# Graph stage: ELUs as relu plus residual plus a clamped exponential, and a row by transposes instead of a matrix product

## What is computed

```python
def _gat(inp, adj_mask, W, a):
    h = jnp.matmul(inp, W)
    f1 = jnp.matmul(h, a[:F_, 0]); f2 = jnp.matmul(h, a[F_:, 0])
    e = jax.nn.leaky_relu(f1[:, :, None] + f2[:, None, :], ALPHA)
    if adj_mask is not None:
        e = jnp.where(adj_mask[None, :, :] > 0, e, NEG_INF)
    att = jax.nn.softmax(e, axis=2)
    return jax.nn.elu(jnp.einsum('bij,bjf->bif', att, h))
out = jax.nn.relu(jnp.matmul(x, mlp1_w) + mlp1_b); residual = out
out = _gat(jax.nn.relu(out), None, W_fc, a_fc)            # 256 features
out = jax.nn.elu(out) + residual
out = jax.nn.relu(jnp.matmul(out, mlp2_w) + mlp2_b); residual = out
out = _gat(jax.nn.relu(out), adj, W_hand, a_hand)         # 128 features
out = jax.nn.elu(out) + residual
return jax.nn.relu(out)
```

## Time and profile before

| | |
|---|---|
| runs, us | 1070.05, 1070.69, 1064.08; median 1070.05 |
| profiled execution, span us | 1059.3 |
| busy, us and share of the span | PE 927.0 (88%), DVE 717.5 (68%), ACT 661.1 (62%), POOL 504.2 (48%) |
| graph stage: b_rden of slot 0 and of slot 13 | 700.4 and 918.4 us from the span's start |
| pace of most full slots | 16.7 us |

### The profile page before, as it was taken

The page is one execution under the profiler, slowest core; times in us unless marked ns, Lnnn a source line. Parts: engine busy times, 40 slices in busy tenths (PEclk is TensorE's granted clock), DMA queues, the critical chain, the costliest instruction groups (busy, mean ns, idle before and its releaser), DMA issues. The chain is left out here.

```text
span 1059.3 us, 25141 instructions
## 1 busy us (share of the span) xinstructions
PE 927.0 (88%) x8021; PEld 805.6 (76%) x8021; DVE 717.5 (68%) x2252; ACT 661.1 (62%) x1691; POOL 504.2 (48%) x498
## 2 busy tenths in 40 slices
PE   1799998999899999999998994798898888768997
PEld 1588887887688999999998993466565666548896
DVE  4599888988464135555554544579898888678775
ACT  4556665654544546666665662688888888867652
POOL 2566564663035564444444442576767732244340
PEclk9999998999699999999999996999999999978999
DMA  7913221211354216777676861011111100000112
GB/s 195 371 50 122 120 109 70 114 42 54 101 148 131 65 49 194 212 202 197 198 200 173 210 162 33 23 33 34 32 35 28 35 6 1 1 1 20 41 42 60
DMA packets 93007, 103.59 MB, mean 98 GB/s; under 512 B 16352, under 2 KB 69856, under 8 KB 90720
## 3 DMA queue, kind: packets, MB, share of 16 engines
q1 hardware_dynamic: 73232, 59.78, 17.3%
q10 hardware_dynamic: 11472, 25.63, 9.0%
q0 software_dynamic: 8192, 16.79, 5.5%
HBM read 52.60 MB, written 43.27 MB: 91 GB/s over the span
## 5 line engine op out<-in xcount | busy, mean ns | idle before, releaser
L1319 POOL DMA_INDIRECT slot_rows_in<-xn_all,slots x128 | 130.1, 1016 | 142.7 <-DMA slot_rows_in<-xn_all,slots 105.8
L1205 ACT ACTIVATE s_hT<-s_hp,expert 128x256 f32<-128x256 f32 x284 | 111.5, 476 | 52.4 <-PE s_hp L1196 52.4
L1218 PE MATMUL s_yp<-w_experts,s_hT 128*128 x1136 | 138.0, 275 | 0.0
L1218 PEld LDWEIGHTS s_yp<-w_experts,s_hT 128*128 128x128 f32 x1136 | 132.8, 192 | 0.0
L1226 DVE TENSOR_TENSOR xnT_all<-s_yp,expert 128x256 f32<-128x256 f32 x71 | 30.2, 425 | 117.9 <-PE s_yp L1218 114.7
L489 DVE SCALAR_TENSOR_TENSOR l_mi<-l_sbc,mT 128x512 bf16<-128x512 f32 x128 | 84.3, 668 | 4.0 <-PE l_sbc L480 3.3
L1194 PE MATMUL s_hp<-e_xh,e_wh 128*128 128x256 f32 x284 | 85.9, 303 | 0.0
L1196 PE MATMUL s_hp<-e_xh,e_wl 128*128 128x256 f32 x284 | 80.1, 282 | 0.0
L1195 PE MATMUL s_hp<-e_xl,e_wh 128*128 128x256 f32 x284 | 80.1, 282 | 0.0
L1176 ACT CAST e_wh<-expert 128x512 fp32r<-128x512 f32 x71 | 43.9, 619 | 48.8 <-issue 43.1
L1120 ACT ACTIVATE s_hT<-s_hp,b_shared 128x512 f32<-128x512 f32 x64 | 42.8, 688 | 48.4 <-PE s_hp L1091 47.2
(11 more groups left out here) (353 smaller groups left out, 2701.0 us busy)
## 6 DMA issues: line engine op xcount, KB each, us to landing
expert<-expert_rows ACTq DMA_DIRECT2D x65, 322.0 KB, 3.4
slot_rows_in<-zeros SPq DMA_DIRECT2D x9, 1024.0 KB, 12.2
xnT_all<-slot_rows_in SPq DMA_DIRECT2D x71, 128.0 KB, 3.4
slot_rows_out<-xnT_all SPq DMA_DIRECT2D x71, 128.0 KB, 2.8
slot_rows_out<-zeros SPq DMA_DIRECT2D x8, 1024.0 KB, 4.4
xn_all<-l_xr SPq DMA_DIRECT2D x16, 256.0 KB, 2.3
xnT_all<-l_rT SPq DMA_DIRECT2D x16, 256.0 KB
out_dram<-xn_all SPq DMA_DIRECT2D x16, 256.0 KB, 2.3
```

The source lines that it names most:

```text
L1205: nc.scalar.activation(hT[q % 2][:, c, :], hp[:, c, 0:TILE], ACT.Gelu, bias=wt[q][:, F + c:F + c + 1]).then_inc(s["h_ok"], 1)
L1218: ins = pe.matmul(yp[q % 2][:, h * D:(h + 1) * D], hT[q % 2][:, c, h * P:(h + 1) * P], w2, start=(c == 0 and h == 0), stop=(c == FC - 1), ...
L1319: pool.indirect_dma_start(k.rows_in, bass.IndirectOffsetOnAxis(ap=k.slots[:, c, b:b + 1], axis=0), k.xn[:, b, :], None).then_inc(scattered ...
```

## The change

Both double ELUs with their residual r are written as max(q, 0) + r + min(exp(exp(q) - 1), 1), which is 1 too much. The cuts of v1 and v2 ahead of the second exponential go. In stage c, DVE does `dve_c_linear` (z1 = max(mm, 0) + r1T) and later `dve_c_sum` (u1 = min(w1, 1) + z1), and POOL's residual goes. In stage e, DVE does `dve_e_sum` (z2 = max(q2, 0) + rr) and `dve_e_out` (s2 = min(w2, 1) + z2). The 1 too much is taken back by constants: mlp2's bias minus the sum of its weights' rows (two small products in `pe_table`, one subtraction), max(s2, 1) for the relu, and -1 in the experts' second bias.

f2 becomes column 129 of h2 (W2C = D + 2), and `pe_d_f2` makes the row from it by four transposes of a broadcast column, after h2 is copied by ACT.

Orders change. DVE's slot now begins e_sum, e_out, c_linear, leaky of d, n_apply, c_sum. ACT does y2's sum after v1 instead of ahead of the rstd step. PE does f2 after `pe_b_sums`, in slot C after the last layer's compaction and row transposes. PE's next writes to `mm` wait for z1 instead of t1.

```diff
-            dve.tensor_scalar(v1[:], v1[:], 1.0, None, ALU.min).then_inc(s["v1_cut"], 1)
...
+        def dve_c_linear(dve, g, p):
+            wait(dve, s["u1_ok"], g)
             wait(dve, s["v1_ok"], g + 1)
+            dve.scalar_tensor_tensor(z1[:], mm[:], 0.0, r1T[p][:], ALU.max, ALU.add).then_inc(s["z1_ok"], 1)
+        def dve_c_sum(dve, g):
+            wait(dve, s["r2_ps"], g)
+            wait(dve, s["z1_ok"], g + 1)
             wait(dve, s["w1_ok"], g + 1)
-            dve.scalar_tensor_tensor(t1[:], w1[:], -1.0, mm[:], ALU.add, ALU.max).then_inc(s["t1_ok"], 1)
-            pool.tensor_tensor(u1[:], t1[:], r1T[p][:], ALU.add).then_inc(s["u1_ok"], 1)
+            dve.scalar_tensor_tensor(u1[:], w1[:], 1.0, z1[:], ALU.min, ALU.add).then_inc(s["u1_ok"], 1)
...
-            pe.matmul(ff[:], k.w_f2_hand[:], r2T[p][:], start=True, stop=True).then_inc(s["f2_ps"], 1)
+            wait(pe, s["h2_ok"], g + 1)
+            for b in range(GB):
+                ins = pe.transpose(ff[:, b * P:(b + 1) * P], h2[:, b, D + 1:D + 2].to_broadcast([P, P]), k.ident[:])
...
-            dve.tensor_scalar(v2[:], v2[:], 1.0, None, ALU.min).then_inc(s["v2_cut"], 1)
+        def dve_e_sum(dve, g):
+            dve.scalar_tensor_tensor(z2[:], q2[:], 0.0, as_batches(rr[:]), ALU.max, ALU.add).then_inc(s["z2_ok"], 1)
         def dve_e_out(dve, g):
-            dve.scalar_tensor_tensor(t2[:], w2[:], -1.0, q2[:], ALU.add, ALU.max).then_inc(s["t2_ok"], 1)
-            dve.tensor_tensor(s2[:], t2[:], as_batches(rr[:]), ALU.add).then_inc(s["s2_ok"], 1)
+            wait(dve, s["x_ok"], g)
+            wait(dve, s["z2_ok"], g + 1)
             wait(dve, s["w2_ok"], g + 1)
+            dve.scalar_tensor_tensor(s2[:], w2[:], 1.0, z2[:], ALU.min, ALU.add).then_inc(s["s2_ok"], 1)
...
         def pe_slot(pe, g, half, p, on):
             if on["d"]:
                 pe_d_h2(pe, g, p)
-                pe_d_f2(pe, g, p)
             if g == C:
                 last.pe_compact(pe, 0)
                 last.pe_row(pe, 1)
+                pe_d_f2(pe, g)
...
             if on["c"]:
                 pe_b_sums(pe, g + 1, q)
+            if on["d"] and g < C:
+                pe_d_f2(pe, g)
...
         def dve_slot(dve, g, half, p, on):
             if on["e"]:
-                dve_e_cut(dve, g - 1)
+                dve_e_sum(dve, g - 1)
+            if on["e"]:
+                dve_e_out(dve, g - 1)
+            if on["c"]:
+                dve_c_linear(dve, g + 1, q)
             if on["d"]:
                 dve_d_leaky(dve, g)
-            if on["c"]:
-                dve_c_cut(dve, g + 1)
             if on["a"]:
                 dve_n_apply(dve, g + 3, q)
             if on["c"]:
-                dve_c_max(dve, g + 1)
-            if on["e"]:
-                dve_e_out(dve, g - 1)
+                dve_c_sum(dve, g + 1)
```

More of the change, by code:

```diff
@@ L1038, in experts_phase @@
         READ_PREFIX = 16
+        W2_SUM = 80
         SPLIT = 2
@@ L1071, in pe_table @@
             pe.transpose(counts[0:EC, 16:16 + J], last_of[:], k.ident[0:J, 0:J])
+            for c in range(2):
+                pe.matmul(counts[:, W2_SUM:W2_SUM + 1], k.w_mlp2[:, c, :], k.ones[:, 0:1], start=(c == 0),
+                          stop=(c == 1), skip_group_check=True)
             for e in range(EXPERTS + 1):
@@ L1541 @@
 W1S = FD + 4
-W2C = D + 1
+W2C = D + 2
 def last_ffn_steps(nc, ctx, k, out, bank, graph, tail_of):
@@ L1659, in pe_row @@
         if g == 0:
-            pe.wait_ge(graph["t1_ok"], GROUPS)
+            pe.wait_ge(graph["z1_ok"], GROUPS)
         wait(pe, s["rank_ok"], g)
@@ L1773, in pe_out @@
         if g < 2:
-            pe.wait_ge(graph[("q2_ok", "s2_ok")[g]], GROUPS)
+            pe.wait_ge(graph[("q2_ok", "z2_ok")[g]], GROUPS)
         wait(pe, s["out_ok"], g - 1)
@@ L1940, in graph_and_last_phase @@
         p1T = sb("p1T", [P, GB * P])
-        v1, w1, t1, u1 = (sb(n, [P, H1, GB * P]) for n in ("v1", "w1", "t1", "u1"))
+        v1, w1, z1, u1 = (sb(n, [P, H1, GB * P]) for n in ("v1", "w1", "z1", "u1"))
         r2T = [sb(f"r2T{p}", [P, GB * P]) for p in range(2)]
@@ L1947, in graph_and_last_phase @@
         p2T = sb("p2T", [P, GB * P])
-        q2, v2, w2, t2, s2 = (sb(n, G4) for n in ("q2", "v2", "w2", "t2", "s2"))
+        q2, v2, w2, z2, s2 = (sb(n, G4) for n in ("q2", "v2", "w2", "z2", "s2"))
         tb = ps("tb", [P, 512])
@@ L2039, in pe_a_dense @@
         def pe_a_dense(pe, g):
-            wait(pe, s["t1_ok"], g - 1)
+            wait(pe, s["z1_ok"], g - 1)
             wait(pe, s["r1_ok"], g * H1)
@@ L2047, in act_a_r1 @@
         def act_a_r1(act, g, p):
-            wait(act, s["u1_ok"], g - 1)
+            wait(act, s["z1_ok"], g - 1)
             for c in range(H1):
@@ L2128, in pe_b_sums @@
             wait(pe, s["r1_ok"], full(lambda n: n * H1, g, 1))
-            wait(pe, s["t1_ok"], g)
+            wait(pe, s["z1_ok"], g)
             wait(pe, s["p1T_ok"], g + 1)
@@ L2142, in act_c_exp, with act_c_exp2 @@
             nc.scalar.activation(v1[:], mm[:], ACT.Exp).then_inc(s["v1_ok"], 1)
-        def dve_c_cut(dve, g):
-            wait(dve, s["v1_ok"], g + 1)
-            dve.tensor_scalar(v1[:], v1[:], 1.0, None, ALU.min).then_inc(s["v1_cut"], 1)
[L2148 to L2154, removed]
-            wait(dve, s["w1_ok"], g + 1)
-            dve.scalar_tensor_tensor(t1[:], w1[:], -1.0, mm[:], ALU.add, ALU.max).then_inc(s["t1_ok"], 1)
-        def pool_c_residual(pool, g, p):
-            wait(pool, s["r2_ps"], g)
-            wait(pool, s["t1_ok"], g + 1)
-            pool.tensor_tensor(u1[:], t1[:], r1T[p][:], ALU.add).then_inc(s["u1_ok"], 1)
+        def act_c_exp2(act, g):
+            wait(act, s["u1_ok"], g)
+            wait(act, s["v1_ok"], g + 1)
+            nc.scalar.activation(w1[:], v1[:], ACT.Exp, bias=k.neg_one[:]).then_inc(s["w1_ok"], 1)
+        def dve_c_linear(dve, g, p):
+            wait(dve, s["u1_ok"], g)
+            wait(dve, s["v1_ok"], g + 1)
+            dve.scalar_tensor_tensor(z1[:], mm[:], 0.0, r1T[p][:], ALU.max, ALU.add).then_inc(s["z1_ok"], 1)
+        def dve_c_sum(dve, g):
+            wait(dve, s["r2_ps"], g)
+            wait(dve, s["z1_ok"], g + 1)
+            wait(dve, s["w1_ok"], g + 1)
+            dve.scalar_tensor_tensor(u1[:], w1[:], 1.0, z1[:], ALU.min, ALU.add).then_inc(s["u1_ok"], 1)
         def pe_c_dense(pe, g):
-            wait(pe, s["s2_ok"], g - 1)
+            wait(pe, s["z2_ok"], g - 1)
             wait(pe, s["r2_ok"], g)
@@ L2242, in pe_d_r2 @@
             wait(pe, s["r2_ok"], full(lambda n: n, g, 1))
-            wait(pe, s["s2_ok"], g)
+            wait(pe, s["z2_ok"], g)
             for b in range(GB):
@@ L2261, in dve_e_quotient @@
         def dve_e_quotient(dve, g, p):
-            wait(dve, s["t2_ok"], g)
+            wait(dve, s["v2_ok"], g)
+            wait(dve, s["z2_ok"], g)
             wait(dve, s["rden2_ok"], g + 1)
@@ L2354, in act_slot @@
                 act_c_exp(act, g + 1)
+            if on["d"]:
+                act_d_sum(act, g)
             if g == B:
```

37 lines of the change are left out of this document (16 added, 21 removed), and 2 rows, old and new, of the table s.

## The result

The change makes the kernel slower: median 1085.99 us (1080.1 to 1091.4, four runs) against 1069.01 us for the kernel before measured beside it (1064.08 to 1070.69), a ratio of 1.0162 with a 95% interval of 1.0115 to 1.021. That is 17.0 us; the forecast was +12.7 and 1082.5. All ratios here leave out runs in a slower state: one of 1078.01 us of the kernel before, and one of 1524.08 us, at a granted clock of 0.564, of the variant with n_apply early. The profiled execution spans 1086.7 us, 27.4 more than that of before, so part of what it shows (some 10 us) isn't the change. The busy times of the page hardly move: PE 925.8, DVE 718.6, ACT 661.8 us, POOL 460.7 for 504.2. So the loss has to be in waits, that is in the pace of the slots.

The account below looks back on a forecast made before the run. No engine is full; a loop through DVE's n_apply, PE and ACT sets the slot. Terms 14.0 + 1.2 - 1.0 - 1.1 - 0.8 + 0.4 = +12.7 on 1070.05 give 1082.75, called 1082.5; range 1068 to 1089, own range 1077 to 1087.

Parts of the forecast that it names:

- slots 1 to 12: Steady graph slots: 16.73 us each becomes 17.96, so 201.48 us becomes 215.5, +14.0.
- slot 0: Graph slot without stage e; c_linear ahead of its leaky group and y2's later sum cost a steady slot's +1.2 us.
- slot -1: Graph slot ahead of slot 0: leaky 1 falls from 1.70 to 0.7 us, -1.0.
- slot 13: Graph slot without n_apply: leaky 1 loses 0.8 us and ACT is 0.3 earlier by the missing cut, -1.1.
- slots 14, 15 and the last phase: Graph stage's end: earlier c_dense gains 2.0 us, slot 15 gives it back; one fewer DVE step in last phase, -0.8.
- experts, start of the graph stage: Experts stage: two small matrix products more cost between 0 and 0.6 us, taken as +0.4.
- rival 3: In 12 slots, e_out with two SBUF inputs waits out 1.0 us of POOL's work: 1094 us, chance 0.16.
- DVE waits for nothing here, with at least 0.15 us to spare: DVE's steps ahead of n_apply: w2, v1 and y2's sum from ACT each arrive before DVE needs them.
- The median of the runs is 10.75 above the span: Whole run: the median's excess over the profiled span of 1059.3 us was taken as unchanged, giving a base of 1070.05.
- Rival 1: Graph slots: c_dense sets the pace, so PE's 0.48 us wait for POOL comes back in 16 slots: 1060, chance 0.10.
- Rival 2: Price paid, but less: cheap c_linear, and PE's clock staying up after shorter idleness wins 2.3 us: 1075, chance 0.16.
- Rival 4: Graph slots: n_apply is later but unseen DVE slack hides it, only the ends (-3) count: 1067 us, chance 0.09.

Follow-up runs that it names:

- the variant with n_apply early: The kernel before with the new ELUs only, DVE doing leaky of d and n_apply ahead of c_linear, e_sum and e_out: 1063.98 us, ratio 0.9932.
- the clean pair: Second profiled executions of the unchanged kernels before and after, on one chip, neither with a late signal: 1058.96 and 1077.11 us, spans 1057.0 and 1075.1.

## Why the prediction was right, and where it was off

**The mechanism held.** DVE's work ahead of n_apply set the pace, PE's wait for n_apply appeared (1.49 us), and leaky 1 takes 0.69 everywhere with 2.93 us of idleness ahead of it. Taking n_apply out from behind the new work, with nothing else changed, gave it all back (16.47 in slots without gathers).

**The slot: 17.96 forecast, 18.14 measured.** n_apply was forecast for R+9.74 and starts at R+9.78; the 0.04 lies between e_sum and e_out, 0.78 from start to start for 0.72. The other steps are as priced: e_out 0.61 to the next start, c_linear 1.14 (and 1.22 long). The larger miss is the hand-over: I let PE start 0.05 behind n_apply's end; it starts at R+11.04, 0.15 behind it. So PE is +1.49 and not +1.35. From there to the next b_rden the kernel gains 0.08, for the forecast 0.12. Twelve times 0.18 is 2.2 us.

**The sum, on the clean pair**, in the order of the prediction, forecast and then measured:

| term | forecast | measured |
|---|---|---|
| slots 1 to 12 | +14.0 | +17.0 |
| slot 0 (b_rden of -1 to b_rden of 0) | +1.2 | +1.6 |
| slot -1 | -1.0 | -1.3 (-0.3 between the first two profiled executions, whose granted clocks there are 0.90 and 0.79) |
| slot 13 | -1.1 | -0.8 |
| slots 14, 15 and the last phase | -0.8 | -0.1 |
| experts, start of the graph stage | +0.4 | +1.8 |
| sum | +12.7 | +18.1 |

The median of the runs moved by 17.0, more than the 12.7 but within the range; at 1085.99 it is 1 us from the upper end of my own range (1077 to 1087), and that it lies inside owes something to luck, as the sum held no term for late signals or the clock. Of the 3.0 in the first line 2.2 are the above, and the rest are slots with gathers (18.19 to 18.82, the last with the fallen clock). The 1.8 at the start is no clean term: it is one execution each, and the same start lies 19.8 us apart between two executions of before. The last phase: c_dense of slot 14 starts 13.07 us behind slot 13's b_rden, before 14.0 and 12.0 by the forecast. The transposes of p2 start 0.33 later than before, and c_dense then waits 0.51 for c_sum, which met POOL's weighing:

```profile
957.29 2.28 DVE L2163 SCALAR_TENSOR_TENSOR g_u<-g_w,g_z 128x1024 f32<-128x1024 f32 x1
...
956.78 1.71 POOL L1653 TENSOR_TENSOR x_tok<-x_tok,xn_all 128x512 f32<-128x512 f32 x1
```

It takes 2.28 us where it takes 1.22 in a slot, and ends 1.08 behind POOL's operation (958.49). (POOL's own takes 1.71 for 1.26; DVE was busy with another operation on two SBUF tensors until 957.37, 0.59 into it.) This is rival 3's mechanism, in the one place where POOL still has such work. By the Trainium skill (SBUF — State Buffer, "Who interferes with whom") two such instructions exclude each other; these two rows agree.

**"DVE waits for nothing here, with at least 0.15 us to spare"** is right in slots 2 to 12 of an execution without late signals, where v1 is done 0.41 to 0.47 us before c_linear starts (slot 11 above), but 0.13 in slot 10. It is wrong in slot 1, where e_out waits 0.91 for w2 and c_linear 0.21 for v1 in both executions of after, and wrong with late signals: c_linear then waits up to 0.97 and the leaky up to 0.34. It is the step that I claimed for all slots from a trace in which no signal was late. That trace could not show it; but so little spare time ahead of a wait deserved a line in the range. Late signals, with the clock, made the profiled execution 7.7 us longer in slots 1 to 12 than the clean one (226.7 and 219.0), with three slots of fallen clock where the clean one has one.

**"The median of the runs is 10.75 above the span"** read as overhead what is spread: a run's time lies only 1.95 above its own span (1088.65 and 1086.7), and runs of before go from 1057 to 1081 us. The sum is not touched by that, as it was added to a median. The bounds that I added up come to 1076 at the lower end; I then wrote 1077.

**The rivals.** Rival 1 (c_dense sets the pace): c_dense doesn't wait for POOL any more and the slot is 1.4 longer, so no. Rival 2 (a smaller price): c_linear takes its full 1.22, and in slot 14 the transposes of p2 still take 1.09 behind 6.04 us of idleness, c_dense 3.75. Rival 3: e_out takes 0.69 in every slot. Rival 4: n_apply came 1.57 later and PE 1.49, so of the 0.23 only 0.08 was slack.

**Left open.** What makes a signal late. Eight of eleven profiled executions with the graph stage's gathers have late signals in their slots, none of three without; two of these three have them in the experts stage, so only those two bear on the gathers. Of the executions whose chip is known, all eight on two chips and the one on a third have them, the three on a fourth don't, so the chip may decide. The recording may have a part in it too: traces with late signals also hold fewer semaphore records (10,474 in the first of after, 13,698 in the second). Which part of an indirect DMA is in the way is open as well; no experiment aimed at any of this. That runs of before hold late signals rests on one profiled execution, 1.8% longer than the other run beside it.

## What to carry to other kernels

Count what stands in an engine's queue ahead of the one operation that another engine's loop waits for, not the work of the engine: the change took 44 us of work from POOL, added next to nothing to DVE, and lost 17 us because 1.5 us of DVE's work a slot lay newly ahead of n_apply. The same ELUs behind n_apply make the kernel 0.7% faster than before. And where an order leaves an engine little spare time ahead of a wait (0.13 to 0.47 us here), look at more than one execution: the less it is, the more of another engine's late signal turns into lost time.

## What the runs showed that I had not expected

- With GpSimd's indirect gathers under way, b_sums' semaphore signal can come 0.70 to 0.84, 1.44 to 1.58 or once 2.26 us behind the end of its matmuls, where 0.01 is usual (a few are 0.06 to 0.17 late). No slot without gathers showed one, also in the two executions that had late signals in the experts stage.
- TensorE's granted clock falls to 0.5 (1.2 GHz of 2.4) for a part of single slots among 1 to 12: in after in slots 2, 5 and 8, with the new ELUs alone in nine of twelve, in the three executions of the kernel before in none. It is no matter of slow kernels alone: the one with n_apply early has one such slot. In slot 5 of after PE had been idle for 2.3 us ahead of its second h1 pair, less than a microsecond before it fell; in slot 8 of the clean execution PE's wait of 1.54 us for n_apply ended 1.8 us before. The same wait stands in slots in which the clock stays up, so it isn't enough by itself. Without gathers such a slot costs 0.63 us more (18.76 for 18.13). No term of my sum held this; the clean execution of after has one such slot (8), so there it is worth some 0.6 us of the 17.
